# Attention scores as products of two fp32r parts in 64-row PE tiles, and the LayerNorm apply on POOL, in a four-block sequence kernel

## The reference

```python
def block0(x, c, ...):                     # block 2 is alike, with rope on q and k
    xm = _modulate(_ln(x), sh_msa, sc_msa)
    q, k, v = ((xm @ W + b).reshape(B, S, 16, 16) for W, b in ...)
    w = softmax(einsum('bqhc,bkhc->bhqk', q / 16, k))
    x = x + g_msa * (einsum('bhqk,bkhc->bqhc', w, v).reshape(B, S, H) @ Wo + bo)
    x = x + g_mlp * (gelu(_modulate(_ln(x), sh_mlp, sc_mlp) @ W1 + b1) @ W2 + b2)
def _ln(x):
    m, v = mean(x), mean((x - m) ** 2)     # over the 256 columns
    return (x - m) * rsqrt(v + 1e-5)
```

## Time and profile before

| | us |
|---|---|
| three timed runs | 1120.85, 1124.29, 1125.54 (median 1124.29) |
| span of the profiled execution, first to last instruction | 1116.0 |
| `att0`, from its first ST to its last PV | 68.5 to 327.1 |
| `att1`, likewise | about 692 to 957.9 |

### The profile page before, as it was taken

How to read it: one execution, slowest core, us unless ns; L and a number is a source line. 1 busy time by engine, 2 the same in 40 slices (tenths; PEclk the granted TensorE clock), 3 DMA queues, 4 the chain that set the end, 5 groups by cost and what they waited for, 6 DMA issues and landing times.

```text
span 1116.0 us, 13198 instructions
## 1 busy us (share of the span) xinstructions
PE 972.8 (87%) x4652; PEld 500.5 (45%) x4652; DVE 655.6 (59%) x983; ACT 445.6 (40%) x786; POOL 458.1 (41%) x538
## 2 busy tenths in 40 slices
PE   3679999999888858878999998999999998798997
PEld 1232332333237747646655553223333232487852
DVE  3758677677825684675223567775756777246223
ACT  1126656566573213200122213665555665532320
POOL 3333343462526646445222157626355004455420
PEclk8789999999999989989999998999999998999988
DMA  7453333333114300120403235323233320000002
GB/s 236 134 159 113 87 124 97 94 103 97 39 40 159 98 7 1 39 76 30 140 1 123 56 99 147 112 85 105 93 91 115 97 68 32 23 11 1 1 1 75
DMA packets 73665, 89.53 MB, mean 80 GB/s; under 512 B 21080, under 2 KB 56224, under 8 KB 73216
## 3 DMA queue, kind: packets, MB, share of 16 engines
q1 hardware_dynamic: 71264, 86.54, 24.6%
q10 hardware_dynamic: 2336, 2.16, 0.8%
HBM read 64.91 MB, written 23.49 MB: 79 GB/s over the span
## 4 chain that ended last, share of the span: by engine, by line
PE 65%; DVE 14%; SPq 5%; ACT 4%; issue 4%; DMA 4%; POOL 3%; ACTq 0%; DVEq 0%; POOLq 0%
PE PS L540 9%; PE PS L518 8%; PE PS L527 6%; PE PS L989 5%; DVE xnorm L339 5%; PE PS L832 5%; PE PS L974 5%; PE PS L852 5%; PE PS L478 5%; SPq L753 4%; PE PS L488 3%; PE PS L499 3%; PE PS L348 2%; DVE U L690 2%; ACT PH L590 2%
## 5 line engine op out<-in xcount | busy, mean ns | idle before, releaser
L690 DVE TENSOR_REDUCE U<-PS 128x2 f32<-128x1024 f32 x256 | 305.4, 1216 | 93.5 <-PE PS L527 91.2
L590 ACT ACTIVATE PH<-PS 128x512 f32<-128x512 f32 x512 | 280.7, 596 | 148.5 <-PE PS L518 146.6
L518 PE MATMUL PS<-U 98*128 98x512 bf16 x512 | 196.9, 390 | 26.9 <-ACT PH L590 16.7
L527 PE MATMUL PS<-U 96*128 96x512 bf16 x512 | 196.0, 395 | 22.3 <-DVE U L690 12.7
L540 PE MATMUL PS<-PH,U 128*32 128x512 f32 x1024 | 138.5, 613 | 2.3 <-ACT PH L590 1.9
L518 PEld LDWEIGHTS PS<-U 98*128 98x128 bf16 x512 | 49.0, 98 | 196.1 <-ACT PH L590 140.6
L339 DVE TENSOR_SCALAR xnorm<-x,mv,rs 128x256 f32<-128x256 f32 x96 | 86.4, 956 | 68.0 <-POOL rs L331 68.0
L989 PE MATMUL PS<-UR,PHR 128*128 128x256 f32 x512 | 104.3, 286 | 12.0 <-DVE tsc L919 6.7
L1062 POOL TENSOR_TENSOR PHR<-PH,PHR 128x512 fp32r<-128x512 f32 x64 | 85.2, 1338 | 71.7 <-ACT PHR L1026 71.3
L327 POOL TENSOR_TENSOR rs<-ve,mhalf 128x4 f32<-128x4 f32 x24 | 24.4, 1019 | 180.8 <-DVE ve L322 180.3
L989 PEld LDWEIGHTS PS<-UR,PHR 128*128 128x128 f32 x512 | 85.5, 194 | 19.7 <-DVE tsc L919 7.9
(11 more groups left out here) (218 smaller groups left out, 1422.4 us busy)
## 6 DMA issues: line engine op xcount, KB each, us to landing
U<-d_parts SPq DMA_DIRECT2D x384, 64.0 KB, 2.2
d_parts<-U SPq DMA_DIRECT2D x32, 384.0 KB, 2.5
d_o<-U SPq DMA_DIRECT2D x32, 256.0 KB, 2.2
U<-in_L_cond_W_dram SPq DMA_DIRECT2D x8, 1024.0 KB, 9.6
W<-in_L_cond_W_dram SPq DMA_DIRECT2D x6, 1024.0 KB, 6.7
U<-d_o SPq DMA_DIRECT2D x32, 128.0 KB
U<-d_rec SPq DMA_DIRECT2D x16, 256.0 KB
gates<-d_gate SPq DMA_DIRECT2D x3, 1024.0 KB, 5.0
```

The lines of the kernel that those rows point to most:

```text
L518: pe.matmul(bank(n % 2), KP[g][0:98, j, kt * P:(kt + 1) * P], QP[g][0:98, j, :], start=True, stop=True).then_inc(self.st_full, 1)
L527: ins = pe.matmul(bank(2 + w % 4), QP[g][0:96, j, qt * P:(qt + 1) * P], KP[g][0:96, j, :], start=True, stop=True)
L590: nc.scalar.activation(PH[:, m % 2, j, :], bank(n % 2), ACT.Exp).then_inc(self.st_read, 1)
L690: v.tensor_reduce(mx[:, G % 2, c:c + 2], PS[:, 2 + (w - 1) % 4:4 + (w - 1) % 4, :], AX.X, ALU.max).then_inc(self.sm_free, 1)
```

## The change

1. **Scores.** q and k are split into two fp32r parts (h, l) instead of three bf16 parts. Q holds h h l and K holds h l h (`SLOTS`), so the products are h·h + h·l + l·h over 48 rows; with the two maximum rows 50. Two heads are stacked in one tile: one from partition 0, one from partition 64. ST(n) uses partitions from 64·(n % 2), SM(n + 28) the other half. The number of score matmuls and their 512 columns stay.
2. **Moves around it.** A save (`WQ`/`WK`) is 3 DMAs of 256 KB instead of one of 384 KB, a `FILL` is 4 DMAs instead of 12, of 48x2x512 fp32, an `MROW` 4 instead of 2. `split_part` ends after two operations per q or k (four with rope) instead of four (six).
3. **LayerNorm.** `norm_rstd` and `norm_apply` become one function `norm_pool` on POOL: one more small operation (minus the mean) and four `tensor_scalar` of 128x256 with two per-partition scalars. DVE's `bn_aggr` waits for the `norm_pool` before it.
4. **Ones rows.** Eight memsets of 2x2048 on POOL or DVE become a memset of 2x512 and four small DMAs for each attention.

```diff
@@ attention's PE step
-                        pe.matmul(bank(n % 2), KP[g][0:98, j, kt * P:(kt + 1) * P], QP[g][0:98, j, :],
-                                  start=True, stop=True).then_inc(self.st_full, 1)
+                        pe.matmul(bank(n % 2), KP[g // 2][r:r + SROWS + 2, j, kt * P:(kt + 1) * P],
+                                  QP[g // 2][r:r + SROWS + 2, j, :], start=True, stop=True).then_inc(self.st_full, 1)
...
-                        ins = pe.matmul(bank(2 + w % 4), QP[g][0:96, j, qt * P:(qt + 1) * P], KP[g][0:96, j, :],
-                                        start=True, stop=True)
+                        ins = pe.matmul(bank(2 + w % 4), QP[g // 2][r:r + SROWS, j, qt * P:(qt + 1) * P],
+                                        KP[g // 2][r:r + SROWS, j, :], start=True, stop=True)
@@ split_part
-                link(eng.tensor_tensor(rest, src, d[:, 0, :], ALU.subtract))
-                link(eng.tensor_tensor(d[:, 1, :], rest, zero, ALU.add))
-                eng.tensor_tensor(d[:, 2, :], rest, d[:, 1, :], ALU.subtract).then_inc(self.split[i], 1)
+                eng.tensor_tensor(d[:, 1, :], src, d[:, 0, :].bitcast(F32), ALU.subtract).then_inc(self.split[i], 1)
@@ FILL
-                        for dst, src, plan in ((QP[g], q, ("000", "11", "2")), (KP[g], k, ("012", "01", "0"))):
...
-                                    sp.dma_start(dst[16 * slot:16 * slot + 16, :, :], s_).then_inc(self.filled[g], 16)
+                        for k, dst in enumerate((QD[g // 2], KD[g // 2])):
+                            src = d_parts[self.a, 4 * b + 2 * (g // 2) + k].rearrange("s d h t -> (s d) h t")
+                            for r in range(2):
+                                sp.dma_start(dst[64 * r:64 * r + SROWS, 2 * (g % 2):2 * (g % 2) + 2, :],
+                                             src[:, 4 * (g % 2) + r:4 * (g % 2) + 4:2, :]).then_inc(self.filled[g], 16)
@@ LayerNorm
-        def norm_rstd(pool, link, k):
+        def norm_pool(pool, link, k, b, waits):
...
+            pool.tensor_scalar(rs[:, 3, :], mv[:, :, 0], -1.0, None, ALU.mult)
...
-        def norm_apply(v, k, b, waits, part=None):
...
             for s, n in waits:
-                v.wait_ge(s, n)
-            for t in tiles(part):
-                ins = v.tensor_scalar(xnorm[:, t, :], x[:, TT * b + t, :], mv[:, t, 0:1], rs[:, 2, t:t + 1],
-                                      ALU.subtract, ALU.mult)
+                pool.wait_ge(s, n)
+            for t in range(TT):
+                ins = pool.tensor_scalar(xnorm[:, t, :], x[:, TT * b + t, :], rs[:, 3, t:t + 1], rs[:, 2, t:t + 1],
+                                         ALU.add, ALU.mult)
```

More of the change, by code:

```diff
@@ L180, in take, with take_r @@
             return ap if dt == F32 else ap.bitcast(dt)
-        QP = [take(1024, BF16).rearrange("p (j t) -> p j t", j=4) for _ in range(4)]
-        KP = [take(1024, BF16).rearrange("p (j t) -> p j t", j=4) for _ in range(4)]
+        def take_r(words):
+            o = at[0]
+            take(words)
+            return UR[:, o:o + words].bitcast(F32), UR[:, o:o + words]
+        QKU = [[t.rearrange("p (j t) -> p j t", j=4) for t in take_r(2048)] for _ in range(4)]
+        QD, KD = [t[0] for t in QKU[0:2]], [t[0] for t in QKU[2:4]]
+        QP, KP = [t[1] for t in QKU[0:2]], [t[1] for t in QKU[2:4]]
         Vt = take(TT * NH * 32).rearrange("p (k h c) -> p k h c", k=TT, h=NH)
-        parts = [take(768, BF16).rearrange("p (c t) -> p c t", c=3) for _ in range(4)]
+        PTU = [[t.rearrange("p (c t) -> p c t", c=2) for t in take_r(1024)] for _ in range(4)]
+        parts_d, parts = [t[0] for t in PTU], [t[1] for t in PTU]
         q32 = [take(T) for _ in range(4)]
-        resid = take(T)
         Osb = [take(T) for _ in range(2)]
@@ L193, in build @@
         mx = take(32).rearrange("p (a c) -> p a c", a=2)
-        mneg = [take(128, BF16).rearrange("p (i c) -> p i c", i=2) for _ in range(2)]
+        MNU = [[t.rearrange("p (i c) -> p i c", i=2) for t in take_r(256)] for _ in range(2)]
+        mneg_d, mneg = [t[0] for t in MNU], [t[1] for t in MNU]
         rt = [take(T) for _ in range(2)]
@@ L674, in dve_task, with set_ones, set_key_ones @@
                 return task
-            def set_ones(self, eng, link):
-                for g in range(4):
-                    link(eng.memset(KP[g][96:98, :, :], 1.0))
+            def set_ones(self, eng):
                 eng.memset(Vt[:, :, :, HD:2 * HD], 1.0).then_inc(self.init, 1)
+            def set_key_ones(self, sp):
+                for i in range(2):
+                    for r in range(2):
+                        sp.dma_start(KD[i][64 * r + SROWS:64 * r + SROWS + 2, :, :],
+                                     ones2[:, :].unsqueeze(1).to_broadcast([2, 4, T])).then_inc(self.kones, 16)
             def dve(self, v, link):
@@ L1771, in att1_ones @@
                 v.wait_ge(low_saved, 128)
-                att1.set_ones(v, link)
+                att1.set_ones(v)
             mlp1.dve(v, link, lambda b: cond_norm(v, link) if b == 0 else None,
@@ L1783, in _ @@
             link = Chain(pool, pool_c)
-            att0.set_ones(pool, link)
-            pool.wait_ge(att0.init, 1)
+            att0.set_ones(pool)
             pool.wait_ge(consts_set, 1)
@@ L1789, in _ @@
             att0.pool(pool, link)
-            mlp0.pool(pool, link, nothing, [lambda: norm_rstd(pool, link, s5.norm0),
-                                              lambda: norm_rstd(pool, link, s5.norm0 + 1)])
+            mlp0.pool(pool, link, nothing, [lambda: norm_pool(pool, link, s5.norm0, 0, [(mlp0.t_full, 2 * B)]),
+                                              lambda: norm_pool(pool, link, s5.norm0 + 1, 1, [(s5.t_full, 2)])])
             s5.pool(pool, link)
@@ L1811, in _ @@
                 sp.dma_start(batch(b), A["x"][b].rearrange("(t p) d -> p t d", p=P)).then_inc(ld_x[b], 16)
+            sp.wait_ge(consts_set, 1)
+            att0.set_key_ones(sp)
             save_gates(sp, 0)
@@ L1877, in _ @@
             sp.wait_ge(low_saved, 128)
+            att1.set_key_ones(sp)
             for j in range(4):
```

100 lines of the change are left out of this document (45 added, 55 removed).

## The result

The changed kernel takes 1182.3 us (median of 4 runs, 1176.2 to 1190.8) where the kernel before takes 1124.3 on the same chip: ratio 1.054, interval 1.049 to 1.059. It is slower by about 58 us. The prediction said 1108, with a range up to 1142, and named a saving: both the direction and the range were wrong.

What follows compares the result with a forecast made beforehand. The prediction took a loop through PE and ACT (3.10 us per group) to bound attention. Its terms, 17 - 9 - 8 - 7 - 14 + 5 = -16, took span 1116.0 to 1100; adding 8.3 gave 1108 us, range 1082 to 1142.

Steps and rivals of the forecast that it cites:

- lie beside a DMA share of 0.29: Costing of saves: twice the bytes saved cost nothing, being beside the low DMA share of `att0`.
- 17 - 9 - 8: Scores part in us: +17 attention loop, -9 earlier first ST in `att0`, -8 shorter fills.
- Start of `att0`, -9: Before the first ST: fewer split operations and fill issues bring ST at 59.5 instead of 68.5, -9 us.
- Fills, -8: Mid-attention: 4 issues instead of 12 free SP; half of DVE's 16.5 us wait for sums reaches PE, -8 us.
- Loop, +17: PE-ACT loop in attention: exposed weight load, +0.11 us for each of 128 groups (+14), and tile-shape switches (+3).
- rival 1: Attention loop: halves overlap fully, SM few ns behind ST; 14 us less in groups, 8 in free stretches; 1086, chance 0.22.
- LayerNorm, -7, -14 and +5: Apply on POOL: -7 us at attention's two ends, -14 in MLP and S5, +5 for POOL lateness at six norms.
- Rival 2: Attention loop: halves don't overlap, ST to SM 0.23 us, switches stay; loop +48 instead of +17, 1139, slower; chance 0.22.
- Rival 3: Split MLPs: POOL becomes the bound, a tile costs 1.0 us, not 0.65; +15 us, 1123, no change; chance 0.10.
- Rival 4: Attention: waits for sums and attention's ends are hidden by the loop; 15 us less gain, 1123, no change; chance 0.08.

## Why the prediction was wrong, step by step

**The step that failed** is the last sentence of its costing: twice the bytes saved "lie beside a DMA share of 0.29". A mean over `att0` says nothing of a queue in which a save has others behind it, and the save was taken as the old one with 1 us more. It landed after 7.2 and 9.2 us instead of some 3.3, since its outer dimension had become 8. The code shows it (`"d h t -> h d t"`), and so does the order on SP, 8x16x512 where 128x1536 stood. I had counted the issues of a save and not read its shape. With 128 rows outermost and all else as in the change, the time is 1107.3.

That this lies by the forecast's 1108 is partly luck. The terms of the scores part were to add up to 0 (17 - 9 - 8) and came to +3.6 in spans, +2.7 in medians, against the LayerNorm part alone. But inside this sum the start brought 4.0 instead of 9, and loop and fills cost 3.6 instead of 9. The end of the kernel, for which there was no term, was 4.9 longer: the same products at a mean granted clock of 0.91 instead of 0.93.

**Start of `att0`, -9.** After: +4.3. With the saves mended: -4.6 to before (63.95), -4.0 to the LayerNorm part alone. The first save then lands at 34.18, as put (34.2). `MROW` leaves at 58.63 instead of the 53.2 of the sum: the second save takes 5.94 where 2.92 stood before, the 13 loads take 9.87 instead of 8.01, and the six issues of a pair of saves take 3.58, since each costs about 0.6 and not the 0.46 of a fill.

**Fills, -8.** Wrong in sign in the changed kernel: the reciprocal's wait rose from 16.5 to 95.1. With mended saves it is 53.2 and with the LayerNorm part alone 54.3, so even there it did not fall. A DVE freed from the apply may arrive at the same reciprocal earlier and wait there instead; that reading is only argued.

**Loop, +17.** Oversized, and rival 1's mechanism was right: 0.01 us from ST to SM, and the group shown takes 3.10, not 3.2. Loop and fills together, forecast +9, came to +3.6 (`att0` +1.4, `att1` +2.2, mended saves against the LayerNorm part alone). If the fills gave nothing, as the wait for the sums suggests, this is 17 less rival 1's 14 for the groups; no run separates the two. Rival 1's further 8 us in the free stretches don't show. Its objection, one unit for weight loads, did not bite: in the changed kernel the loads of two halves start 0.03 us apart or less (316.45 and 316.48), 0.18 us each.

**LayerNorm, -7, -14 and +5.** The sum of -16 was about right: -12.6 in spans, -19 in medians. In the stages: `att0` +0.3, `att1` -4.8, between them -6.1, the end -1.4. A tile on POOL takes 0.559 at the median against my 0.65, and four on the chain 2.15 to 2.19 in most places (3.6 in two) against my 2.6. POOL's lateness showed where it was put, larger than its +5 but within its 0 to +20: in the changed kernel PE waits 21.2 us for L1066, 5.3 before.

**The clock** had no term. The sum counted stalls once; of the 73.8 us that the slow saves cost in the span, 37.9 are products at a lower granted clock.

**Which rivals.** None held the outcome; no rival had a slower save. Rival 1 had the loop right and not the time. Rival 2 forecast a slower kernel, but by a mechanism that fell (0.01 us from ST to SM and not 0.23). Rival 3 fell with 0.559 us for a tile. Rival 4 held that the waits for sums are hidden by the loop: in the three versions with a later reciprocal they were not, 15 to 30 us came back. With the kernel before itself this was not tried.

## What to carry to other kernels

When a save's order of dimensions changes, read the outermost one of both patterns and the DMA share within a 2 us window of that transfer; a mean share over a stage hides a queue at half width. A late transfer in an in-order queue can cost twice, once as a wait and once as clock; here it was 35.9 and 37.9 us. Price a saving on an engine by what else in its loop then waits: here some 13 us less product time in each attention bought nothing, since PE waited for ScalarE instead. The best kernel of the study has the old scores, the LayerNorm of the change and the reciprocal six steps later: 1089.6 us, 0.969 of before (0.966 to 0.973).

## What the runs showed of the hardware

- Saves of 256 KB in 2 KB pieces: 202 to 205 GB/s at a share of 0.52 to 0.53 with 8 outermost, 361 to 387 GB/s at 1.01 to 1.03 with 128.
- `fp32r` products over 48 and 50 rows in the two 64-row halves start 0.00 to 0.01 us apart; where nothing holds them up, the next pair starts 0.34 us after the pair ahead (315.20 to 315.54). In series within one half the products start 0.33, 0.24 and 0.23 us apart, so the first pair takes 0.57. Four up to PV take 1.15 in series and 0.83 side by side, a short wait for ScalarE included.
- PV on 32-column tiles: two heads hold PE for 0.99 us, and four heads for 0.99 us.
- An apply of 128x256 takes 0.55 to 0.56 us on POOL at the median, and on DVE 0.93 at the median and 0.388 at the least.
- A save of 384 KB with 8 outermost lands after 6.54 and 6.66 us, where 2.27 and 2.92 stood with 128.
